# Sorting 412,500 graph edges on one core: one-hot matmul permutation of 3,328 edges at a time, and scatters of 8-record segments

## The reference, cut to what matters

```python
edge_index = jnp.stack([src, dst])
h = jnp.maximum(_layernorm(x, axis=-1), 0.0)
x = x + _L0_gnn_ref(h, edge_index, L0_gnn_weight)          # h[src], h[dst] per edge, sums by src
h = jnp.maximum(_layernorm(x, axis=-1), 0.0)
x = x + _L1_gnn_ref(h, edge_index, edge_attr_4, ...)       # h[src], h[dst], edge_attr per edge, sums by src
```

## Time and profile before

| what | value |
|---|---|
| median of three executions | 18632.32 us |
| the profiled execution's own time | 18678.13 us |
| its span, first to last instruction | 18676.4 us |
| granted TensorE clock, mean over the span | 0.602 of 2.4 GHz |
| busy: GpSimd, VectorE, TensorE, ScalarE | 11232.0, 7621.0, 4883.5, 2249.7 us |
| scatters of the sort (L607) | 3224, from 762.30 to 4925.9 us |
| packets moved by DMA | 770968, 1143.50 MB |

### The profile page before, as it was taken

One profiled execution on the slowest core, in us unless ns is written; L12 is line 12 of the kernel. 1 busy time (PEld: TensorE's weight loads), 2 busy tenths in 40 slices (PEclk: granted clock), 3 DMA queues, 4 the chain that ended last, 5 costly groups with the idle time before them and its releaser, 6 DMA issues. The chain is left out here.

```text
span 18676.4 us, 142664 instructions
## 1 busy us (share of the span) xinstructions
PE 4883.5 (26%) x28224; PEld 3607.4 (19%) x28225; DVE 7621.0 (41%) x14277; ACT 2249.7 (12%) x4882; POOL 11232.0 (60%) x12446
## 2 busy tenths in 40 slices
PE   0000000000011111111111982323232222228997
PEld 0000000000000000000000881111111111113996
DVE  5879600000133333333333884333333333336775
ACT  2000000000000000000000880000000000005333
POOL 0267777777666656656564763666666666640773
PEclk6555555555555555555555995565556665669998
DMA  2000000000122222222224441222222222257331
GB/s 52 3 4 5 5 5 5 5 5 5 35 71 73 69 68 72 73 66 71 66 75 55 151 133 40 67 64 69 64 67 66 66 67 64 69 71 233 106 106 58
DMA packets 770968, 1143.50 MB, mean 61 GB/s; under 512 B 322012, under 2 KB 469339, under 8 KB 770652
## 3 DMA queue, kind: packets, MB, share of 16 engines
q1 hardware_dynamic: 386972, 666.22, 11.7%
q0 software_dynamic: 322304, 245.26, 8.5%
q10 hardware_dynamic: 61632, 231.44, 3.1%
HBM read 872.56 MB, written 269.54 MB: 61 GB/s over the span
## 5 line engine op out<-in xcount | busy, mean ns | idle before, releaser
L1343 POOL DMA_INDIRECT big<-b_d,big x3424 | 3278.0, 957 | 2288.8 <-POOLq L140 1251.0
L868 POOL DMA_INDIRECT big<-h_d,big x3424 | 3279.6, 958 | 1945.9 <-issue 1100.7
L607 POOL DMA_INDIRECT rec_d<-big x3224 | 3098.5, 961 | 1599.3 <-issue 983.1
L910 PE MATMUL ps<-big 128*128 x3424 | 746.8, 373 | 8842.1 <-PEq L140 5339.8
L910 PEld LDWEIGHTS ps<-big 128*128 128x128 bf16 x3424 | 441.7, 162 | 9147.0 <-issue 9146.7
L929 DVE TENSOR_REDUCE ps<-ps 128x260 f32<-128x780 f32 x856 | 837.7, 979 | 3249.9 <-remote 1349.6
L1470 DVE TENSOR_REDUCE ps<-ps 128x256 f32<-128x768 f32 x856 | 827.5, 967 | 2530.8 <-DVEq L140 1417.1
L1669 POOL TENSOR_SCALAR big<-iota_f,big 128x128 f32<-128x128 f32 x1498 | 875.1, 604 | 842.6 <-DMA big<-rec_d 527.3
L1422 PE MATMUL ps<-big 128*128 x3424 | 608.4, 335 | 2764.4 <-issue 2318.4
L628 DVE CAST big<-big 128x896 f32 (+2 forms) x9 | 8.3, 918 | 2778.3 <-DMA big<-h_d 2777.3
L1422 PEld LDWEIGHTS ps<-big 128*128 128x128 bf16 x3424 | 442.9, 159 | 3124.0 <-issue 3123.9
(11 more groups left out here) (350 smaller groups left out, 10074.8 us busy)
## 6 DMA issues: line engine op xcount, KB each, us to landing
big<-e_d SPq DMA_DIRECT2D x428, 512.0 KB, 3.2
rows_d<-big ACTq DMA_DIRECT2D x214, 544.0 KB
big<-rows_d SPq DMA_DIRECT2D x214, 544.0 KB, 3.3
HA<-slots_d SPq DMA_DIRECT2D x214, 512.0 KB
big<-slots_d SPq DMA_DIRECT2D x214, 512.0 KB
e_d<-big ACTq DMA_DIRECT2D x214, 512.0 KB
big<-rec_d SPq DMA_DIRECT2D x860, 64.0 KB, 3.0
big<-h_d,big POOLq DMA_INDIRECT x3424
```

What stands on the lines that cost most here:

```text
L607: gp.indirect_dma_start(rec_d, bass.IndirectOffsetOnAxis(ix_stage[b][:, j:j + 1], 0), rec_stage[b][:, j * REC:(j + 1) * REC], None).then_i ...
L868: gp.indirect_dma_start(G[g][:, t * ROW:(t + 1) * ROW], None, h0_d, bass.IndirectOffsetOnAxis(idx[g % 2][:, t:t + 1], 0)).then_inc(gath[g] ...
L910: m = t.matmul(XS[q % 2][:, n, 0:3 * D + 3], OT3[g % 2][:, o, :], T0[:, ds(chunks[o // 2] * TW, 3 * D + 3)], start=True, stop=True)
L1343: gp.indirect_dma_start(G[g][:, t * D:(t + 1) * D], None, b_d, bass.IndirectOffsetOnAxis(idx[g % 2][:, t:t + 1], 0)).then_inc(gath[g], 16)
```

## The change

**The order.** A chunk's records are rounded up to a whole number of tile pairs with 7 more places than before; the number of blocks is 214 again. `rec_d` now holds the records in their order, tile by tile (row i is record i). A second array, `rec2_d`, has the old layout; the first gather stage reads `rec_d` through `rec_tile` (128 x 16 rows of 32 bytes a block), writes each block as it is to `rec2_d` (128 rows of 512 bytes), waits for that before it reloads the buffer, and the later stages read `rec2_d`.

**The sort.** The 3,224 columns are taken in 124 supertiles of 26 columns (3,328 edges; J = 26, NS = 124). In a supertile the records of a chunk are put together and padded to a multiple of 8, which fills at most 512 segments of 8 records (L = 8). Where an edge goes is a segment (0 to 511) and an offset in it (0 to 7). TensorE permutes: for each quarter w of the segments and each column j it multiplies a one-hot matrix of segments (`DH`, 128 x 128, bf16) with a row of 15 values times the one-hot of the offset (`EX`, 120 columns: slot, two parts of dst, three bf16 parts of each of four attributes). The sums in PSUM are 128 segments of 8 whole records, and GpSimd scatters 128 segments of 256 bytes with one indirect DMA. Segments of a supertile may overhang into the place of the next one's records, so GpSimd waits for the scatters of the supertile before. `rank_span`, its integer operations, and ScalarE's staging are gone.

A supertile on VectorE is, in this order: `n_i`, a shift, a copy and the scan `INC` (99 columns each), `A2` (198) and `ANC`; `prod` (2,574), `gpos` and `STEP`; `sel`, a reduction of 2,574; five operations on 26 columns and the one-hot of offsets (208); `flags` (2,574), `before` (comparison, product and reduction of 338) and `attributes` (five linked operations on 104) for the next supertile; 18 of the 26 segment one-hots (512 each; ScalarE makes the other 8 by Square and Relu); three operations on 400 elements; and `take_out` of the supertile before, four operations on 4, 32, 64 and 384 elements. Cut to its core:

```diff
-        for pieces in SPANS:
-            w = pieces * RB
-            rank_span(c0, w)
-            ...
+def flags(b, s):                       # B3: which chunk, 128 x 26 x 99, bf16
+    n = go(v.tensor_tensor(B3[b], iota_b[:, 0:NC].unsqueeze(1).to_broadcast([P, J, NC]),
+                           S[:, ds(s * J, J)].unsqueeze(2).to_broadcast([P, J, NC]), ALU.is_equal))
+def before(b, s):                      # same4, 128 x 338: equal chunks; times `earlier`; reduced to wp
...
+def attributes(b):                     # 5 linked operations on 104 columns: three bf16 parts
...
+def take_out(b):                       # from Y (PSUM): 4, 32, 64 and 384 elements
+    consume(v, y_rdy)
...
+    v.sem_inc(y_free[b], 1)
+    v.sem_inc(st_rdy, 1)
+def supertile(b, s, first=False, last=False):
+    consume(v, rt_rdy)
+    need(go(v.tensor_scalar(n_i, n_all, float(L - 1), None, ALU.add)))
...
+    n = go(v.tensor_tensor(prod..., B[b]..., A2.unsqueeze(2).to_broadcast([P, 2, GJ, NC]), ALU.mult))
...
+    n = go(v.tensor_reduce(sel, prod.rearrange("p (j c) -> p j c", c=NC), AX, ALU.add))
...
+    v.sem_inc(seg_rdy, 1)
+    need(go(v.tensor_tensor(OHL[b], ..., ALU.is_equal)))        # 208
+    v.sem_inc(l_rdy, 1)
+    if not last:
+        flags(1 - b, s + 1)
+        before(1 - b, s + 1)
+        attributes(1 - b)
+    for j in range(J - ACTD):          # 18 of 512 columns, bf16
+        n = go(v.tensor_scalar(DH[b][:, j * WS:(j + 1) * WS], iota_w, seg_f[b][:, j:j + 1], None, ALU.is_equal))
+    hits = ...                         # 400, then product 400, reduce 400
+    if not first:
+        take_out(1 - b)
+    go(v.tensor_tensor(dest[b], dsum, g8, ALU.add))
```

```diff
 @block.tensor
+def ranks(b):                          # 13 + 13 + 13 + 26 = 65 matmuls of 99 columns into RT
+    consume(t, b_rdy)
...
+def place(b):
+    consume(t, y_free[b]); consume(t, e_rdy); consume(t, d_rdy); consume(t, da_rdy)
+    for w in range(NW):                # 4
+        t.matmul(o, ones_b, crow[...], start=True, stop=False)
+        for j in range(J):             # 26
+            m = t.matmul(o, DH[b][:, j * WS + w * P:j * WS + (w + 1) * P],
+                         EX[b][:, j * CH * L:(j + 1) * CH * L], start=False, stop=(j == J - 1))
+with t.Fori(0, NS // 2 - 1) as i:
+    for b in range(2):
+        ranks(1 - b)
+        place(b)
 @block.scalar
+for n in range(ACTD):                  # 8: Square, then 8: Relu, of 512 columns, for the other DH
 @block.gpsimd
+def spread(b, s):
+    consume(gp, l_rdy); consume(gp, pa_rdy); consume(gp, e_free[b])
+    gp.tensor_tensor(EX4[b][:, :, 0:3, :], PC..., OHL[b]..., ALU.mult).then_inc(e_done, 1)      # 624
+    gp.tensor_tensor(EX4[b][:, :, 3:CH, :], PA[b]..., OHL[b]..., ALU.mult).then_inc(e_done, 1)  # 2496
+def scatter(b, s):
+    consume(gp, st_rdy)
...
+    for w in range(NW):
+        gp.indirect_dma_start(rec_d, bass.IndirectOffsetOnAxis(ix[b][:, w:w + 1], 0),
+                              stage[b][:, w * L * REC:(w + 1) * L * REC], None).then_inc(scat, 16)
+with gp.Fori(1, NS // 2) as i:
+    for b in range(2):
+        spread(b, i * 2 + b)
+        scatter(1 - b, i * 2 + (b - 1))
```

```diff
 # before the supertiles, VectorE: passes over 3224 columns for the values that are permuted
+link(v.tensor_scalar(lo_i, s_i, P - 1, None, ALU.bitwise_and))
+link(v.tensor_scalar(PC[:, :, 0], lo_i, 1.0, None, ALU.add))
...
 # first gather stage, SyncE
-    sp.dma_start(rec[g], rec_blk[g]).then_inc(rec_in[g], 16)
+    sp.dma_start(rec3[g], rec_tile[g]).then_inc(rec_in[g], 16)
...
+    sp.dma_start(rec2_blk[ds(k, 1), :, :].rearrange("k p w -> p (k w)"), rec[g]).then_inc(kept[g], 16)
...
     consume(sp, rec_free[g])
+    consume(sp, kept[g], 16)
-    sp.dma_start(rec[g], rec_blk[ds(k + 4, 1), :, :].rearrange("k p w -> p (k w)")
+    sp.dma_start(rec3[g], rec_tile[ds(k + 4, 1), :, :, :].rearrange("k p t w -> p (k t) w")
```

More of the change, by code:

```diff
@@ L345, in build @@
         top[0] = 0
[L346 to L357, removed]
@@ new lines, in build @@
+        JNC = J * NC // 2
+        B = [HA[:, 3 * COLS + b * JNC:3 * COLS + (b + 1) * JNC].bitcast(BF16) for b in range(2)]
+        assert 3 * COLS + 2 * JNC <= NC * (D + AGW)
+        B3 = [x.rearrange("p (j c) -> p j c", c=NC) for x in B]
+        prod = take(J * NC)
+        attb = [take(J * 4) for _ in range(2)]
+        rem = take(J * 4)
+        PA = [take(J * 12 // 2, BF16).rearrange("p (j q a) -> p j q a", q=3, a=4) for _ in range(2)]
+        OHL = [take(J * L // 2, BF16).rearrange("p (j l) -> p j l", l=L) for _ in range(2)]
@@ new lines, in build @@
+        same = take(2 * GJ * GJ // 2, BF16)
+        same4 = same.rearrange("p (g j k) -> p g j k", g=2, j=GJ)
+        earlier_f = take(GJ * GJ)
+        earlier = take(GJ * GJ // 2 + 1, BF16)[:, 0:GJ * GJ]
+        wp = [take(J) for _ in range(2)]
+        sel, seg_f, l_f = take(J), [take(J) for _ in range(2)], take(J)
+        q_i, sg_i, l_i = (take(J, I32) for _ in range(3))
+        stage = [take(NW * L * REC) for _ in range(2)]
+        stage4 = [z.rearrange("p (w l c) -> p w l c", l=L, c=REC) for z in stage]
@@ new lines, in build @@
+        ix = [take(NW, I32) for _ in range(2)]
+        ACTD = 8
+        apart = [[take(WS // 2, BF16) for _ in range(ACTD)] for _ in range(2)]
+        iota_w = take(WS // 2, BF16)
+        crow = take(NW * CH * L // 2, BF16)
+        crow4 = crow.rearrange("p (w c l) -> p w c l", c=CH, l=L)
+        tri_b, ones_b = take(P // 2, BF16), take(P // 2, BF16)
+        n_i = take(NC, I32)
+        n8, gpos = take(NC), take(NC)
+        INC, ANC, STEP = take(NC + 1), take(NC + 2), take(NC + 1)
+        hit = take(NW * (NC + 1))
@@ L424, in _ @@
+                with sp.Fori(0, FULL // 2) as i:
+                    for b in range(2):
+                        load(b, i * 2 + b)
+                load(0, FULL - 1)
+                for s in range(FULL, NS):
+                    b, n = s % 2, max(LASTE - s * J, 0)
+                    consume(sp, att_free[b])
+                    rest(b, s)
                     if n > 0:
+                        sp.dma_start(attb[b][P - 1:P, n * 4:J * 4], zeros[0:1, 0:(J - n) * 4]).then_inc(s_z, 16)
+                        sp.wait_ge(s_z, 16)
+                        e0 = (P - 1) * COLS + s * J
@@ new lines, in _ @@
+                v.tensor_copy(ones_b, ones[:, :])
+                v.tensor_copy(earlier, earlier_f)
+                v.memset(crow, 0.0)
+                for z in stage:
+                    v.memset(z, 0.0)
+                link(v.tensor_copy(tgrid, tgrid_i))
+                for c, value in enumerate((-1.0, float(N // P * P), float(N % P))):
+                    v.memset(crow4[0:1, :, c, :], value)
+                v.memset(ANC[:, 0:1], 0.0)
+                v.memset(ANC[:, NC + 1:NC + 2], float(DUMP + MID))
@@ L472, in _ @@
[L472 to L479, removed]
+                link(v.tensor_tensor_scan(incl, tiles, zc, 0.0, ALU.add, ALU.add))
+                link(v.tensor_tensor(gpos, incl, tiles, ALU.subtract))
@@ new lines, in _ @@
+                for b in range(2):
+                    v.sem_inc(att_free[b], 1)
+                flags(0, 0)
+                before(0, 0)
+                attributes(0)
+                supertile(0, 0, first=True)
+                supertile(1, 1)
+                with v.Fori(1, NS // 2 - 1) as i:
+                    for b in range(2):
+                        supertile(b, i * 2 + b)
+                supertile(0, NS - 2)
+                supertile(1, NS - 1, last=True)
+                take_out(1)
@@ L610, in release @@
[L610 to L621 removed]
+                    gp.sem_inc(pa_free[b], 1)
@@ L854, in _ @@
                     sp.wait_ge(rec_in[g], 16)
+                for g in range(NBLK % 4):
+                    sp.wait_ge(kept[g], 16)
             @block.gpsimd
```

390 lines of the change are left out of this document (232 added, 158 removed).

## The result

The changed kernel takes 17956.3 us (median of 4 runs, 17951.6 to 17968.4) against 18634.0 before (four executions): a ratio of 0.9638, 95% interval 0.9621 to 0.9654, or 678 us less. The forecast was 18360. The profiled execution took 17952.67 us, its span is 17950.9 us.

What follows compares the result with a forecast made beforehand. VectorE was to bound the sort: 23.8 us of work plus 8.0 held by GpSimd's products, paid 124 times. 18678.1 (profiled) - 324 (sort) + 50 (gathers) = 18404, or 18360 for the median; 8-in-10 range 17380 to 18900.

Steps and rivals of the forecast that it cites:

- The scatters stop being the bound: Sort: 496 DMAs instead of 3224, at 1.26 us each 625 us, or 5.0 us a supertile, no longer the bound.
- VectorE's own work, 23.8 us: Sort: the sum of VectorE's operations for one supertile, 23.8 us, before any holding by GpSimd.
- I take it that they are held ... for all of the 8.0 us: Sort: VectorE's operations are locked out while GpSimd makes the two products for `EX`, adding 8.0 us to each supertile.
- three streams at the memset's rate: Price of GpSimd's products: two inputs and one output at the memset's rate, 2.5 ns an element, 8.0 us with fixed cost.
- T: Sort: the time of one supertile, paid 124 times, forecast as 23.8 + 8.0 = 31.8 us.
- Head and tail: Around the sort's loop: it starts at about 640 us; 27 us follow it before the load of `h_d` at 4610.
- TensorE and ScalarE hidden: Sort: TensorE (9 to 28 us) and ScalarE (some 10 us) a supertile stay under 31.8 us, beside VectorE.
- The gather stage, +50: First gather stage: smaller reads, an extra write and the wait for it add 50 us for the start and collisions.
- No hold: Rival, sort: products lie beside VectorE's work, supertile 24 us, total 17390 us; chance 0.25 together with half a hold.
- The products' own price: Rival, sort: GpSimd's products cost more, 4 ns an element giving 18920 us, 4.7 ns giving 19190; chance 0.17.
- no hold or half a hold: Rival range, sort: VectorE is held not at all or for part of the products, 17390 to 18000 us; chance 0.25.
- The gather stage, +400: Rival, gather stage: it gets slower by 400 us in place of 50, total 18710 us; chance 0.05.

## Why the prediction was right in kind and short in size

**The scatters stop being the bound:** right. 496, 0.97 us each, and GpSimd waits in front of them.

**VectorE's own work, 23.8 us:** right, 23.6 in the changed kernel less its holding, 23.94 with the products moved away. The earlier trace rows had one size only and could not tell 1.04 ns an element from 0.155 us of fixed cost; 2.83 us for 2574 elements against 1.22 for 1024 give both. All large terms are within 0.1 us: `prod` 2.83, `sel` 2.83, `flags` 2.84, 18 one-hots 4.82.

**"I take it that they are held ... for all of the 8.0 us":** the mechanism is right, the size is the step that failed. The products take 4.40 + 1.24 = 5.64 us, not 8.0. Of my bounds, 4.7 ns an element (from an operation of 128, with its fixed cost) was nearly three times too high and 0.85 two times too low. My "three streams at the memset's rate" should have been two: 1.7 ns, not 2.5. The Trainium skill's figure (GPSIMD Engine Reference, section 3.1), from which I had estimated 6.9 us, is for fp32; fp32 measured 2.25 ns here, near its 2.2, and bf16 is cheaper.

**The rest of the difference:** the small product starts inside `flags` and mostly waits instead of holding, so 4.9 of 5.64 us are paid, and not all of it as I had supposed. T is 28.53 instead of 31.8: 2.36 us less for the price of the products, 0.75 for the part that is waited and not held, 0.16 for VectorE's own work. Against the sum's 18404 the profiled 17952.67 is 451 us less: 3.27 x 123 = 402 from the period, 17 from head and tail, 33 from the gather stage. (The profiled execution of before stood 46 us over its median, that of after 4 under it, so 404 of it show in the medians.)

**Head and tail:** the loop starts at 638.7 (640 said). The seven passes took 16.1 us (18 said). From the start of the last supertile to the load are 43 us, where the forecast has 31.8 + 27 = 59: this supertile has no `flags`, `before` and `attributes` and takes VectorE 22 us, and what stands behind it takes 21, not 27. The load came 419 us before 4610.

**TensorE and ScalarE hidden:** right. Place takes four times 1.5 to 2.8 us, the rank sums 5.4, at a granted clock of 0.68 on average from 640 to 4200 us; ScalarE takes 9.3. Doubling, halving and moving the products moved the period by VectorE's share each time, so nothing else stood near 28.5, and at 21.8 still nothing did.

**The gather stage, +50:** about right, smaller. From the load to the end the profiled executions differ by 17.4 us on the first chip (743 - 726) and 16.7 on the last (658.7 in the sort, 642.0 in all, with the small rows read twice). A second read added nothing to it that shows, which speaks against the number of small reads as its cause; whether it is the wait for the write or something else was not tried. The stage was also longer before than I had it: 5161.5 us from its first gather to its last, 24.1 us a block and not 23.6, which changes nothing in the sum.

**The rivals.** "No hold" is out: the hold is there whenever VectorE has a held kind beside a product. Its counter-evidence was sound for what it showed: of the 1926 comparisons of 128 on VectorE (267 to 541 ns, median 277), 967 began inside one of GpSimd's own comparisons of 128 (588 to 694 ns) by the spans of the trace, and 292 of these ended before it did. So a short operation on GpSimd holds VectorE for less than its whole span; that the hold lasts to the end is shown for products of 312 to 2496 elements and for the memsets of the earlier trace rows. "The products' own price" was the right term with the wrong sign: it was cheaper, not dearer. The time fell where I had put "no hold or half a hold" (17390 to 18000, 0.25), though the hold is whole: a cheaper product gives the same time. "The gather stage, +400" is out by the rows above.

## What to carry to other kernels

VectorE and GpSimd are two engines only for some kinds of work. Before moving elementwise work to GpSimd, sort VectorE's operations into held kinds (two inputs in SBUF, casts, an input in SBUF and a constant) and free kinds (reductions, an input in PSUM), and let GpSimd start when a free stretch of its length begins: here that alone was worth 559 us, with the same operations in another order. And when a new bound is a sum on one engine, price the neighbour that holds it with a probe of the same type and size; a sum right to 0.2 us is worth little beside one term that is off by 2.4.

## What the runs showed of the hardware

- A GpSimd product of bf16 costs 1.7 to 1.9 ns an element, of fp32 2.25; copy and memset 0.9. An input that repeats over 8 elements is no dearer.
- The hold covers tiny operations too: an int32 shift of 26 elements took 3.70 us beside a product.
- Issuing a scatter is held as well. In the kernel with both products beside `prod` they fall beside `flags`, of two SBUF inputs, and the issue that is normally 0.96 us takes 2.49. The mean over 458 scatters is 1.36 us there, 0.97 in the changed kernel, where they fall beside `prod`:

```profile
2012.62 2.84 DVE L561 TENSOR_TENSOR HA<-iota_b,HA 128x2574 bf16<-128x2574 bf16 x1 [0.27 <-DVE big L639]
2013.80 2.49 POOL L781 DMA_INDIRECT rec_d<-big  x1 [0.30 <-issue]
```

- The same program differs by 10% between chips (18634 us on one, 16816 to 16852 on three others), most of it in the two stages of gathers: the first takes 5162 us on one and 4344 on another, the second 5293 and 4335. The changed kernel's sort ends at 4191.1 us on both.
